# A two-layer graph network on one core: the exps of a row block in two passes of 2048 columns in place of four of 1024

## What is computed

```python
# layer 0
mask = (adj > 0)
agg = mask @ x / maximum(sum(mask, 1), 1)
x = layernorm(x + relu(concat(x @ W_self + b_self, agg @ W_nb + b_nb) @ W_comb + b_comb))
# layer 1
neib_att = tanh(neigh @ Wn1 + bn1) @ Wn2 + bn2          # 4096 x 32
value = neigh @ Wv + bv                                 # 4096 x 128
x_att = tanh(x @ Wx1 + bx1) @ Wx2 + bx2                 # 4096 x 32
ws = leaky_relu(x_att @ neib_att.T, 0.01)               # 4096 x 4096
ws = softmax(where(adj > 0, ws, -9e15), axis=1)
x = layernorm(x + concat(x @ Wfx + bfx, ws @ value))
```

## Time and profile before

| what | value |
|---|---|
| runs (3) | 885.54, 885.69, 886.63 us; median 885.69 us |
| the profiled execution | 887.7 us |
| its span, first to last instruction | 885.9 us |
| mean granted clock of the tensor engine | 0.975 of full speed (2.4 GHz) |
| instructions | 17654 |
| ScalarE busy | 512.6 us |
| exps (L652) | 128 of 1147 ns |
| DMA | 120.27 MB, mean 136 GB/s |

### The profile page before, as it was taken

One profiled execution on the slowest core, in us unless ns is written; L12 is line 12 of the kernel. 1 busy time (PEld: TensorE's weight loads), 2 busy tenths in 40 slices (PEclk: granted clock), 3 DMA queues, 4 the chain that ended last, 5 costly groups with the idle time before them and its releaser, 6 DMA issues.

```text
span 885.9 us, 17654 instructions
## 1 busy us (share of the span) xinstructions
PE 760.1 (86%) x6224; PEld 600.5 (68%) x6224; DVE 655.7 (74%) x1599; ACT 512.6 (58%) x937; POOL 354.8 (40%) x364
## 2 busy tenths in 40 slices
PE   0579699968999999999999999999998899999885
PEld 0445354646777777777777777777777777777664
DVE  0557644547888888888888888888888888888674
ACT  0024232216666666666666666666666666666694
POOL 0000010155455545555555555555555555555301
PEclk9889699989999999999999999999999999999999
DMA  9700230297666676766766776666666666764000
GB/s 301 260 1 1 67 75 0 42 232 173 157 162 162 157 168 156 161 155 156 162 161 159 162 165 160 158 165 158 166 165 157 156 155 155 156 157 91 13 13 12
DMA packets 175384, 120.27 MB, mean 136 GB/s; under 512 B 140608, under 2 KB 158912, under 8 KB 175296
## 3 DMA queue, kind: packets, MB, share of 16 engines
q1 hardware_dynamic: 171856, 117.63, 54.3%
q10 hardware_dynamic: 3440, 1.51, 0.6%
HBM read 81.37 MB, written 4.19 MB: 97 GB/s over the span
## 4 chain that ended last, share of the span: by engine, by line
PE 64%; DVE 21%; ACT 6%; issue 5%; ACTq 2%; POOL 1%; DMA 1%; DVEq 0%; POOLq 0%
PE ps_v L831 10%; PE ps_t L818 9%; PE ps_agg L795 8%; PE ps_agg L798 8%; PE ps_v L834 5%; DVE score L501 5%; PE ps_s L809 4%; PE ps_s L777 3%; DVE p_both L547 3%; ACT score L645 2%; PE ps_x L851 2%; PE ps_x L848 2%; ACT p_both L658 2%; ACTq L595 2%; DVE l L523 2%
## 5 line engine op out<-in xcount | busy, mean ns | idle before, releaser
L831 PE MATMUL ps_v<-v,p_both 128*128 128x256 f16 x1024 | 199.0, 273 | 59.5 <-DVE res L565 58.8
L645 ACT ACTIVATE score<-ps_s,sc 128x512 f32<-128x512 f32 x256 | 177.2, 692 | 118.3 <-PE ps_s L809 118.1
L501 DVE CUSTOM_DVE_ANT_0 score<-score,bias 128x512 f32<-128x512 f32 x256 | 196.0, 765 | 65.9 <-ACT score L645 62.4
L795 PE MATMUL ps_agg<-y,mask_t 128*128 128x257 f16 x1024 | 240.8, 274 | 0.0
L798 PE MATMUL ps_agg<-y,mask_t 128*128 128x256 f16 x1024 | 235.7, 273 | 0.2 <-DMA mask_t<-mask 0.2
L348 POOL TENSOR_SCALAR bias<-mask 128x1024 bf16<-128x1024 bf16 x128 | 160.9, 1257 | 172.6 <-DVE mask L469 158.4
L658 ACT CAST p_both<-ps_t 128x512 f16<-128x512 f32 x256 | 149.0, 582 | 99.5 <-PE ps_t L818 95.2
L547 DVE TENSOR_TENSOR p_both<-ps_t,p_both 128x512 f16<-128x512 f32 x256 | 174.8, 683 | 39.9 <-ACT p_both L658 37.0
L834 PE MATMUL ps_v<-v,p_both 128*128 128x128 f16 x1024 | 180.0, 220 | 4.3 <-DVE p_both L547 4.2
L831 PEld LDWEIGHTS ps_v<-v,p_both 128*128 128x128 f16 x1024 | 100.3, 98 | 103.9 <-issue 70.1
L818 PE MATMUL ps_t<-ident,score 128*128 128x128 f32 x1024 | 154.4, 273 | 2.0 <-ACT score L652 2.0
(11 more groups left out here) (117 smaller groups left out, 766.9 us busy)
## 6 DMA issues: line engine op xcount, KB each, us to landing
adj_sb<-in_adj_dram SPq DMA_DIRECT2D x128, 512.0 KB, 4.3
z<-in_L_gnn_neigh_dram SPq DMA_DIRECT2D x8, 512.0 KB, 9.2
score<-in_x_dram SPq DMA_DIRECT2D x8, 512.0 KB, 9.9
x_in<-in_x_dram SPq DMA_DIRECT2D x32, 128.0 KB, 4.0
out_dram<-out_sb SPq DMA_DIRECT2D x32, 128.0 KB, 2.1
mask_t<-mask SPq DMA_TRANSPOSE x128, 3.2
bias<-in_L_gnn_W_comb_dram ACTq DMA_DIRECT2D x1, 512.0 KB, 5.5
bias<-in_L_gnn_W_self_dram ACTq DMA_DIRECT2D x1, 256.0 KB, 3.7
```

Of the source, the lines that this page charges most:

```text
L501: dve.tensor_tensor_reduce(score[:, b % 2, part], score[:, b % 2, part], bias[:, b % BIAS_BUFS, part], 1.0, -3.0e38, ALU.add, ALU.max, par ...
L645: act.activation(score[:, b % 2, k * GW:(k + 1) * GW], ps_s[k % 2][:, :], ACT.Prelu, alpha=SLOPE, scale=score_scale).then_inc(leaky_made, 1)
L795: mm = pe.matmul(agg[:, 0:D + 1], mask_t[:, c, :], y16[:, c, 0:D + 1], start=(c == 0), stop=(c == NC - 1), skip_group_check=True)
L831: mm = pe.matmul(ps_v[:, 0:2 * DV], p_hi[:, k % 2, chunk], v16[:, c, :], start=(c == 0), stop=(c == NC - 1), skip_group_check=True)
```

## The change

Each row block's exps are done in two instructions of 2048 columns, in slots 23 and 27. The ones in slots 25 and 29 are gone. `sums` has two columns for each block in place of four, and the waits that count exps (in row_max, layer1 and turn_p) count two for each block: the transposes of groups 0 and 4 wait for an exp, in place of those of groups 0, 2, 4 and 6. Nothing else is moved.

```diff
+EW = 2048
+NE = N // EW
...
-        sums = sb("sums", [P, 2, NQ], F32)
+        sums = sb("sums", [P, 2, NE], F32)
...
-                at_least(dve, exp_made, NQ * (b - 1))
+                at_least(dve, exp_made, NE * (b - 1))
...
-                dve.wait_ge(exp_made, NQ * (b + 1))
+                dve.wait_ge(exp_made, NE * (b + 1))
...
-                part = score[:, b % 2, q * QW:(q + 1) * QW]
+                part = score[:, b % 2, q * EW:(q + 1) * EW]
...
                 if d := due(s, ROW_MAX_AT + 1):
-                    if d[1] % 2 == 0:
-                        exps(d[0], d[1] // 2)
+                    if d[1] % (NG // NE) == 0:
+                        exps(d[0], d[1] // (NG // NE))
...
             def turn_p(b, k):
-                if k % 2 == 0:
-                    pe.wait_ge(exp_made, NQ * b + k // 2 + 1)
+                if k % (NG // NE) == 0:
+                    pe.wait_ge(exp_made, NE * b + k // (NG // NE) + 1)
```

## The result

The changed kernel takes 959.67 us (median of 4 runs, 956.54 to 959.81) against 886.16 us for the kernel before on the same chip (4 runs, 885.54 to 887.08). The ratio is 1.082, with a 95% interval of 1.080 to 1.085. The forecast was 958.4 us. In the profiled execution the span went from 885.9 to 957.9 us.

The account below looks back on a forecast made before the run. A loop of tensor engine, ScalarE and VectorE down to L565 was taken to set each block's time; 67.2 us (even stretch), 1.7 (beginning), 2.85 (end) and 1 (clock) made 72.7 us more, so 958.4 us, range 912 to 968.

Parts of the forecast that it names:

- The loop: Each block: scores of slot 22, ScalarE, VectorE down to L565, tensor engine; the first exp's end lies on it, +0.85 us.
- The exp: ScalarE: 1024 more columns cost 0.85 us, so a 2048-wide exp takes 2.00 us in place of 1147 ns.
- the saved fixed parts: ScalarE: 64 fixed parts of about 0.3 us saved, 19 us in all, buying nothing where it waits for the tensor engine.
- The stall: Tensor engine waiting for L565: grows from 1.87 to about 2.7 us, +0.85 us a block.
- The second exp: Slot 27, beside the loop: costs nothing, covered by 0.82 us of idle time before the Prelu, nearly used up.
- The clock: Behind each block's longer stall the tensor engine's clock falls to half speed, costing 1.55 us a block (nothing to 1.7).
- The stall of 2.91 us: Stall ending at 182.45 in the earlier trace, clock 0.50 behind it; taken as nearest to the forecast 2.7 us.
- the rule of the Trainium skill: Rival: throughput drops only from longer idle gaps, so no clock fall behind the longer stall; 914 us, chance 0.16.
- The sum: Even stretch, beginning, end and clock falls there: 72.7 us on 887.7, giving 960.4, less 2.0 for the median: 958.4 us.
- Even stretch: 28 of the 32 row blocks, 235 to 837 us: 28 x (0.85 + 1.55) = 67.2 us.
- Beginning: Exps of the first two blocks, each 0.85 us on the path: 1.7 us.
- End: Last two blocks, behind 837 us, without aggregation to cover ScalarE: 2.85 us; clock falls at beginning and end 1 us.

Follow-up runs that it names:

- first_narrow: Changed kernel with the first half of the row in two exps of 1024 (slots 23, 25), the second exp still 2048 wide (slot 27): 887.58 us.
- second_narrow: Changed kernel with the first exp still 2048 wide (slot 23), the second half in two exps of 1024 (slots 27, 29): 957.15 us.
- dve_delay: Kernel before, four narrow exps kept, with one more VectorE instruction of 752 columns ahead of layer1 in blocks 0 to 29: 955.87 us.
- first_1536: Three exps a block of 1536, 1536 and 1024 columns (slots 23, 26, 29) in place of the changed kernel's two: 937.85 us.
- shift3_narrow: Kernel before, four exps, with transposes, values and layer1 of a block three slots later (27, 28, 36): 861.15 us.
- shift3_wide: Changed kernel, two exps of 2048, with transposes, values and layer1 three slots later: 891.77 us.
- shift3_wide_last: Changed kernel with transposes, values and layer1 three slots later and each exp issued behind its slot's cast and Prelu: 874.65 us.
- shift3_wide_mixed: Changed kernel, transposes, values and layer1 three slots later, only the first exp behind its slot's cast and Prelu, the second ahead of them: 864.44 us.
- shift3_narrow_last: Kernel before, four exps, transposes, values and layer1 three slots later, each exp behind its slot's cast and Prelu: 858.51 us.
- fill12: Changed kernel with 12 extra matmuls of 252 columns inside the tensor engine's stall in blocks 1 to 29: 913.07 us.

## Why the prediction was right

**The loop.** It went as read: first exp, cast, subtraction, masked scores, layer0, layer1, stall. `first_narrow` (no loss), `second_narrow` (69.6 of 73.5 us) and `dve_delay` (69.2 us without a wide exp) leave little else.

**The exp.** 2003 ns measured, 2.00 us forecast from the slope between the two Copy forms. The whole chain moved by 0.85 us. That the saved fixed parts buy nothing is shown by `first_narrow`, which saves 32 of them and takes the same time.

**The stall.** 2.58 us, forecast about 2.7. The transposes of slot 24 came 0.08 us later after the start of the exp (+2.14 against +2.06), as forecast, and the scores of slot 25 0.13 later (+5.70 against +5.57), so the tensor engine started to idle later.

**The second exp.** Its cover of 0.82 us was used up and sufficed; no wait of the tensor engine appeared in slots 27 and 28.

**The clock.** This was the choice that decided the number. The stall of 2.91 us was the nearest case and a good guide; a block lost 23.89 - 21.48 - 0.85 = 1.56 us by the fall, forecast 1.55, for the reason given there, that a bit of the slow stretch falls on idle time. That both terms came out so exactly is partly luck. A fall that lies wholly behind the resumption cost 1.67 us (24.00 - 22.33 in `second_narrow`, below), and the share that falls on idle time could not be read from the rows. Nor does the length of the stall alone decide: the changed kernel has one of 2.56 us before its even stretch, ended by the first exp, and the clock stays at 1.00 behind it.

```profile
211.48 0.66 PE L820 MATMUL ps_t<-ident,score 128*128 128x128 f32 x4 [2.56 <-ACT score L654]
```

The prediction went by length alone and had no term for this; in the even stretch of the changed kernel it did not show. By the rule of the Trainium skill that the prediction weighed (TensorE: Matmul & The Clock Gate, "Why this matters for your kernels"), a stall of this length would still have been safe and the time 914 us. The trace does not agree: in the even stretch, behind stalls of 2.58 us, the clock fell in 28 blocks out of 28.

**The sum.** Even stretch (resumptions of 28 blocks, by the ends of L565 and L567): 668.8 us after 601.8, 67.0 more, forecast 67.2. Beginning (start of the first L567 against L565): 237.58 against 235.53, 2.05, forecast 1.7; 0.60 of it is there before the first exp (183.05 against 182.45 at the first of the long stalls), so the exps account for 1.45. End (behind the 29th of them): 2.9 us, forecast 2.85 and 1 for the clock; no fall was added at either end, so the 1 us was not there. In all 72.0 us more span against 72.7. Between the medians it is 73.5 us. The agreement within 1 us owes something to luck, since a bound of 0 to 1.7 us a block stood behind the largest term.

Expectations failed in `first_1536`, by the share of blocks with a fall, and in the rebuilt kernels, there mostly by the same step: I named the wait that goes and not the one that is late next. In `shift3_narrow` three short ones remained, in `shift3_wide` the exp's delay met the subtraction of slot 24 and not the x1 transposes, in `shift3_wide_last` the second exp met the tanh. `shift3_wide_mixed` was right in the even stretch and missed what the stalls of the last blocks do.

## What to carry to other kernels

Merging instructions on an engine that mostly waits saved nothing here, and let the instructions queued right behind the merged one start later by the whole added length; look up what is queued there and how much idle time it has, exp by exp, as the same instruction cost 70 us in one slot and nothing in the other. When a change lengthens a stall of the tensor engine, price the clock behind it from the longest stalls that the trace already shows, even if they lie in the prologue; that part was more than half of the loss here (28 x 1.56 = 44 of 73 us). Give it a chance and not a certainty, as stalls of one length went either way. A little useless work in such a stall can be worth more than it costs (46.6 us here), but removing the stall is better (shift3_narrow_last, 101 us under the changed kernel).

## What the runs showed of the hardware

- The stall behind which the clock falls, in the even stretch: 1.87 us, never in 28; 2.29 us, in 22 blocks of 28; 2.58 us (changed kernel) and 2.72 us (`dve_delay`), in each of 28; 2.60 us (`second_narrow`), in 27 of 28.
- The length alone does not decide. Stalls of 2.56 us (changed kernel, 211.48), 2.59 us (`second_narrow`, 239.46), 2.66 us (`dve_delay`, 924.63) and 2.54 us (`shift3_narrow`, 827.65) had no fall behind them. What else decides was not tested.
- The block time settles at 23.89 us, and the traces show how. `second_narrow` has all the stages; its first three resumptions:

```profile
239.46 0.27 PE L836 MATMUL ps_v<-v,p_both 128*128 128x256 f16 x1 [2.59 <-DVE res L567]
261.79 0.27 PE L836 MATMUL ps_v<-v,p_both 128*128 128x256 f16 x1 [2.59 <-DVE res L567]
285.79 0.27 PE L836 MATMUL ps_v<-v,p_both 128*128 128x256 f16 x1 [2.60 <-DVE res L567]
```

  The first block has no fall and takes 22.33 us, which is 21.48 + 0.85. The next has its fall wholly behind the resumption, 0.89 us after it, and takes 24.00 us. In the even stretch two falls in a row are always 23.89 us apart here, so with each block the fall begins 0.11 us sooner after the resumption. Once it begins ahead of it, part of the slow stretch is spent idle and the block gets shorter, down to 23.89 us with the fall 0.16 us ahead; there it stays. The changed kernel comes to the same state from the other side (0.36 us ahead and a block of 23.79 us at first), and so does `dve_delay`, from 24.00 us. In that state a stall 0.14 us longer did not lengthen the block. In `first_1536` (23.57 us with a fall) the rhythm cannot hold, and every fifth or sixth block has no fall. This is read off the traces; no run was made for it.
- With work in the stall the tensor engine resumed sooner after the last reader of the bank: 0.06 us after the end of L567 (505.67 + 0.35 to 506.08) in `fill12`, 0.15 us after it (524.45 to 524.60) in the changed kernel.
